# An output bias added to the residual stream beforehand by GpSimd, and a row of maxima sent ahead of a stack of parts

## The reference

```python
x = x + layernorm(attn0(layernorm(x)))            # phase one: 16 heads of 8, causal
f = layernorm(x)
for l in range(2):                                # l = 0: phase two, l = 1: phase three
    f = f + attn(ln(f, ln1[l]), wq, wk, wv, wo, bq, bk, bv, bo)   # the residual: f + y @ wo + bo
    h = ln(f, ln2[l])
    moe = token_moe if l == 0 else seq_moe        # 8 experts, the best 2 for a token / a sequence
    f = f + moe(h)
x = x + layernorm(f)
```

## Time and profile before

| | before |
|---|---|
| time, median of 3 runs | 1253.86 us (1253.05 to 1258.78) |
| the profiled execution's own time | 1253.16 us |
| its span, first to last instruction | 1251.4 us |
| TensorE's matmuls busy | 1060.6 us (85%) |
| VectorE busy | 980.6 us (78%) |
| ScalarE busy | 792.0 us (63%) |
| GpSimd busy | 685.8 us (55%) |

### The profile page before, as it was taken

One profiled execution on the slowest core, in us unless ns is written; L12 is line 12 of the kernel. 1 busy time (PEld: TensorE's weight loads), 2 busy tenths in 40 slices (PEclk: granted clock), 3 DMA queues, 4 the chain that ended last, 5 costly groups with the idle time before them and its releaser, 6 DMA issues. The chain is left out here.

```text
span 1251.4 us, 37899 instructions
## 1 busy us (share of the span) xinstructions
PE 1060.6 (85%) x10453; PEld 789.4 (63%) x10453; DVE 980.6 (78%) x2919; ACT 792.0 (63%) x1908; POOL 685.8 (55%) x1018
## 2 busy tenths in 40 slices
PE   1788999999999999999369997388889889989997
PEld 0565666666666666666269997255656556658986
DVE  3678999999998898899547765368888998876665
ACT  1566777777777767776158886256666666754554
POOL 3345555556656777776723333566676676532332
PEclk9999999999999999999679999589999899989999
DMA  5232111111111221121122222243311212100000
GB/s 144 86 110 78 50 38 42 51 52 53 53 40 45 68 66 52 55 66 43 36 72 67 69 67 74 57 116 99 85 53 53 64 39 67 53 2 10 23 18 21
DMA packets 118053, 73.07 MB, mean 58 GB/s; under 512 B 8384, under 2 KB 112960, under 8 KB 117952
## 3 DMA queue, kind: packets, MB, share of 16 engines
q1 hardware_dynamic: 99296, 53.11, 15.3%
q10 hardware_dynamic: 14560, 10.35, 3.0%
q0 software_dynamic: 4096, 8.40, 2.1%
HBM read 21.68 MB, written 11.60 MB: 27 GB/s over the span
## 5 line engine op out<-in xcount | busy, mean ns | idle before, releaser
L617 DVE TENSOR_REDUCE negm<-bank 128x2 f32<-128x512 f32 (+1 forms) x576 | 389.3, 679 | 82.0 <-PE bank L309 57.0
L505 ACT ACTIVATE prob<-bank 128x512 f32<-128x512 f32 x576 | 339.6, 595 | 127.1 <-PE bank L331 88.8
L898 POOL TENSOR_SCALAR_AFFINE_SELECT prob<-prob 128x512 f32<-128x512 f32 x384 | 248.6, 649 | 172.6 <-ACT prob L505 170.7
L350 PE MATMUL bank<-prob,vaug 128*32 128x256 f32 (+1 forms) x3072 | 168.6, 338 | 4.1 <-ACT oT L511 3.3
L1217 POOL COPY w_job<-w_s 128x512 f32 x104 | 69.1, 665 | 153.4 <-PE bank L1186 152.6
L317 PE MATMUL bank<-stack 126*128 126x256 bf16 x768 | 151.8, 279 | 0.0
L336 PE MATMUL bank<-stack 128*128 128x256 bf16 x768 | 150.8, 278 | 0.9 <-ACT prob L505 0.9
L1208 ACT ACTIVATE prob<-bank,b_job 128x128 f32<-128x128 f32 (+1 forms) x416 | 131.8, 400 | 17.2 <-PE bank L1186 9.9
L1197 PE MATMUL bank<-w_job,prob 128*128 128x128 f32 x1088 | 139.0, 276 | 2.5 <-issue 1.6
L1197 PEld LDWEIGHTS bank<-w_job,prob 128*128 128x128 f32 x1088 | 131.3, 192 | 6.4 <-issue 5.3
L350 PEld LDWEIGHTS bank<-prob,vaug 128*32 128x32 f32 x3072 | 81.5, 110 | 80.7 <-issue 48.9
(11 more groups left out here) (181 smaller groups left out, 2122.0 us busy)
## 6 DMA issues: line engine op xcount, KB each, us to landing
stack<-parts SPq DMA_DIRECT2D x288, 128.0 KB
w_s<-e_w ACTq DMA_DIRECT2D x32, 256.0 KB, 3.0
oT<-x_routed SPq DMA_DIRECT2D x72, 64.0 KB, 1.7
y_routed<-oT SPq DMA_DIRECT2D x36, 128.0 KB, 1.9
stack<-mT SPq DMA_DIRECT2D x192, 4.0 KB
out<-x_all SPq DMA_DIRECT2D x16, 128.0 KB, 1.8
b_all<-e_b ACTq DMA_DIRECT2D x2, 512.0 KB, 8.4
x_routed<-hk,x_at POOLq DMA_INDIRECT x64
```

Of the source, the lines that this page charges most:

```text
L350: m = nc.tensor.matmul(o, w, (prob0, prob1)[kb][:, g % 2, h], start=kb == 0, stop=kb == 1, skip_group_check=True)
L505: nc.scalar.activation(o, s, ACT.Exp, scale=SCALE).then_inc(exp_done, 1)
L617: nc.vector.tensor_reduce(o, s, AX.X, ALU.max, negate=True).then_inc(max_done, 1)
L898: nc.gpsimd.affine_select(out=t, in_=t, compare_op=ALU.is_ge, fill=0.0, base=0, pattern=[[0, HG], [1, P]], channel_multiplier=-1).then_inc ...
```

## The change

GpSimd gets a new instruction for each item of phases two and three, `pool_bias`, in slot 3 of the step before the item's own: it adds the output bias to the item's part of `f_all` in place. The residual of these items on VectorE becomes one instruction, PSUM plus `f_all`, in place of two. `res` is advanced by two at once, so later waits are as before. In slot 2, SP sends all six stack DMAs of an item of phases two and three after the row of maxima; for items of phase one, two still go ahead of it. The placing pieces 3, 4 and 5 move from slot 3 to the middle of slot 2, the end of slot 2 and the beginning of slot 3.

```diff
         def dve_residual(i):
 
-            base = NRES * i.v
             dve.wait_ge(o3_ps, i.v + 1)
+            if i.phase > 0:
+                dve.wait_ge(biased, i.v - B + 1)
+                nc.vector.tensor_tensor(pair(f_all, i), post_bank[:, 0:T].rearrange("p (j d) -> p j d", j=2),
+                                        pair(f_all, i), ALU.add).then_inc(res, 2)
+                return
             nc.vector.tensor_tensor(att[:, i.par], post_bank[:, 0:T].rearrange("p (j d) -> p j d", j=2),
                                     bo_s[:, i.phase:i.phase + 1].to_broadcast([P, 2, P]),
                                     ALU.add).then_inc(res, 1)
-            if i.phase > 0:
-                dve.wait_ge(res, base + 1)
-                nc.vector.tensor_tensor(pair(f_all, i), pair(f_all, i), att[:, i.par], ALU.add).then_inc(res, 1)
...
             if k == 3 and placing:
-                dve_place(first, 3)
+                dve_place(first, 5)
...
+            if k == 2 and placing:
+                dve_place(first, 3)
             if k == 2 and ranked:
                 dve_logits(oldest)
...
+            if k == 2 and placing:
+                dve_place(first, 4)
             if k == 2 and ranked:
                 dve_top(oldest, 0)
             if k == 3 and ranked:
                 dve_top(oldest, 2)
-            if k == 3 and placing:
-                dve_place(first, 4)
-            if k == 3 and placing:
-                dve_place(first, 5)
...
+        def pool_bias(i):
+
+            pool.wait_ge(xn_ok, 2 * i.v + 2)
+            alone(pool)
+            nc.gpsimd.tensor_tensor(pair(f_all, i), pair(f_all, i),
+                                    bo_s[:, i.phase:i.phase + 1].to_broadcast([P, 2, P]), ALU.add).then_inc(biased, 1)
...
             if ie:
                 pool_select(ie, ge, 1)
+            if k == 3 and nxt and nxt.phase > 0:
+                pool_bias(nxt)
...
+            ahead_of_row = 2 if nxt and nxt.phase == 0 else 0
             if k == 2 and nxt:
-                sp_stack(nxt, range(0, 2))
+                sp_stack(nxt, range(0, ahead_of_row))
             if im:
...
             if k == 2 and nxt:
-                sp_stack(nxt, range(2, 6))
-            if k == 3 and nxt:
-                sp_stack(nxt, range(6, TERMS))
+                sp_stack(nxt, range(ahead_of_row, TERMS))
```

More of the change, by code:

```diff
@@ L201, in build @@
         top, placed, rank_ps, hk_sb = sem("top"), sem("placed"), sem("rank_ps"), sem("hk_sb")
+        biased = sem("biased")
         x_sent = [sem("x_sent0"), sem("x_sent1")]
```

## The result

| | before | after |
|---|---|---|
| time, median of 4 runs each | 1255.51 us (1253.05 to 1258.78) | 1287.59 us (1285.09 to 1291.89) |
| the profiled execution's own time | 1253.16 us | 1291.89 us |
| ratio after / before, 95% interval | | 1.026 [1.022, 1.030] |

The changed kernel is slower, by 32 us in the medians and by 39 us between the two profiled executions. The sign was as forecast, the size was not: 1264 us was predicted, and the range ended at 1275.

A forecast was written before the change was run, and what follows sets the result against it. The stack was taken to bound items 15 to 20, VectorE's slot 1 items 38 to 44, both nearly items 21 to 30. Terms 7.1 + 4.9 - 4.5 + 2.2 + 2.1 - 1 = +10.8 on 1253.16 gave 1264 us, range 1250 to 1275.

The forecast's parts named there:

- SP's order decides: SP's queue, phases two and three: a step lasts the end of `mT` plus 8.05 us, unless something else is later.
- A: Items 15 to 20, six steps, bound by the stack: from 17.0 to 18.2 us each, +7.1 us.
- B: Items 21 to 30, ten steps, bound by stack and VectorE nearly at once: 18.45 us each, +4.9 us.
- D: Items 38 to 44, seven steps, bound by VectorE in slot 1: from 19.6 to 18.65 us each before a clock allowance.
- Six DMAs in 7.1 us: Step's end: from the first of six stack DMAs to TensorE's start takes 7.1 us, with bounds of 6.9 and 7.37.
- So I give 2 back: Items 38 to 44: TensorE's single stack waits of some 2 us bring half clock, cutting the gain from 6.5 to 4.5 us.
- Rival 3: Longer waits halve the clock often: from item 15 on, 0.5 us more for 20 steps, 1274 us; chance 0.13.
- Items 38 to 44, -4.5 us: VectorE's slot-1 bound goes and the stack bounds these seven steps: 4.5 us gained after 2 us given back for the clock.
- The two additions become one: VectorE's residual: one instruction of 0.41 us; VectorE gains 1.16 us in items 21 to 30, 2.18 in 38 to 44.
- GpSimd's bias costed at nothing: End of GpSimd's slot 3: the new addition takes 0.58 us, none on the path; uncovered, 19 us over 32 items.
- Placing at nothing: Small instructions moved about one slot forward from the end of slot 3 cost nothing, in time VectorE has freed.
- C, +2.2 us: Items 32 to 37, six steps while second-layer expert weights load: 19.9 us a step, 119.4 in all, 2.2 us slower.

The follow-up runs named there:

- e1: The kernel before with SP's new order alone, all six stack DMAs after the row in phases two and three: 1310.09 us, ratio 1.043.
- e2: The changed kernel with SP's old order, two stack DMAs ahead of the row for every item: 1257.82 us, ratio 1.002.
- e3: The changed kernel with seven filler matmuls before TensorE's wait for the stack in phases two and three: 1270.76 us, ratio 1.012.
- e5: e2 with six filler matmuls before TensorE's wait for the row of group 1 in phases two and three: 1259.35 us, ratio 1.005.
- e11: The changed kernel without GpSimd's bias, which is left out of the output for phases two and three: 1288.92 us, ratio 1.026.
- e8: e5 without GpSimd's bias, which is left out of the output for phases two and three: 1252.11 us, ratio 0.999.
- e4: The kernel before with GpSimd's bias and the joined residual alone, SP's order and placing pieces as before: 1259.63 us, ratio 1.004.
- e6: The changed kernel with one stack DMA ahead of the row in phases two and three, in place of none: 1255.20 us, ratio 1.000.
- e12: The changed kernel with the bias behind GpSimd's fetches, SP's old order, and six filler matmuls before the row wait, items 22 to 44: 1247.17 us, ratio 0.992.

## Why the prediction was right in its sign and wrong in its size

**SP's order decides: right.** e1 and e2 show it from both sides. With the old order the change makes no difference, with the new order alone it loses 54 us. The form of the step, `mT` plus row plus six DMAs, held in every step of A, B and D.

**Six DMAs in 7.1 us: mis-sized.** They took 7.58 on average, near the 7.37 of the earlier trace rows, which I had as the upper bound. I had taken the value from four DMAs plus two issues. With the clock kept (e3) they took 7.36 over the same steps, so the half clock explains about half of the excess and no more. With a row to first DMA that took 0.92 to 1.3 us in most steps of B and D instead of 0.75, set against an earlier `mT` (9.97 for 10.4, 10.49 for 10.6), this makes e3's span, at full clock, 5.8 us longer than my forecast's, and 7.8 without the 2 us that I had given for the clock. The Trainium skill's figure ("DMA: Bandwidth & Descriptors", Anatomy of one DMA), by which I had estimated about 6.2 us for six, was further off than the rows. It stands there for DMAs that GpSimd issues, which my prediction did not say, and these are SP's.

**"So I give 2 back": this is the step that failed.** I priced the half clock in D alone and at 2 us, where e3's filler alone takes back 16.8 us, most of it in B and C. The row to look at was my own: I wrote that TensorE would wait for the stack about 2 us in one piece and that waits of this size had come with the half clock, and then let that count in one stretch, although the same wait stood at the end of every step from A on. Rival 3 had the mechanism, at 0.5 us for 20 steps; it was 1.6 us for some ten, and with the DMAs' longer time it carries the result past the range. Its "against", that item 17 waited and ran at 1.00, rested on a wait of 0.61 us, which says nothing of waits of 2. None of my signs of being wrong watched the clock.

**Items 38 to 44, -4.5 us: +3 off, and for another reason than I gave.** They gained 1.4. The seven steps were to lose a bound by VectorE. Item 42 in the kernel before shows that there was none: 18.78 us with the blocked L675 in it, at full clock. What D had to gain was the half clock of five of its steps, and the changed kernel won most of that back (0.94 to 0.99), while the stack cost it 0.3 us a step.

**The two additions become one: right** as a duration, 0.415 us in all 32 cases, never blocked. The rule that the Trainium skill gives ("SBUF — State Buffer", Who interferes with whom) agrees with this, and again with the combine in e5, which has two inputs in SBUF and stretched from 0.62 to 1.89 us for two beside GpSimd's L920.

**GpSimd's bias costed at nothing: right in the changed kernel, wrong beyond it.** e11 measures nothing there, e8 measures 7 us with the old order. It was 0.72 us rather than 0.58, and what the waits for `y_got` in e5 and e8 point to is the fetch behind it in its queue, not the next step's parts. I had named sends and fetches as queued behind it and not followed who waits for them.

**Placing at nothing: right**, as far as e4 against e2 can tell.

**C, +2.2 us: mis-sized** for the same two reasons, 11.4 in the event, of which 8.1 went away with e3's filler. **The drain, -1:** the rest of the span is 0.4 longer and not shorter.

Left open: why in B the first stack DMA leaves 1.29 us after the row in some steps, where nothing in the queue stands between; why waits of 1.96 us and more went with half clock at ten steps of the five stretches and not at two others, while in e2 shorter ones, from 1.62 us, were enough; and what in the six DMAs takes the time that four did not show.

## What to carry to other kernels

Before you put a small transfer ahead of a large one in a queue, look at what the small one is waiting for, because the large one will wait for it too: here two of six DMAs could leave 1.2 us earlier than the row, and holding them back cost 54 us over 31 steps (e1). With one of them left ahead (e6) the changed kernel's loss was gone. When a forecast says that TensorE will wait in one piece, multiply by the steps and price the slower clock behind each of those waits, from the longest waits of the trace and not from its average ones. And when an instruction that was blocked is made fast, compare steps that ran with and without the slower clock before booking its time as a gain.

## What the runs showed of the hardware

- The granted clock fell to 1.2 GHz with ten waits of 1.96 to 5.83 us for the stack in the changed kernel, and in e2 also behind waits from 1.62 us for the row. One such stretch made a slot of 4.65 us into one of 6.23. Six or seven matmuls whose result nobody reads, placed before the wait, kept the clock at 1.00 in B and D (e3, e12; in C it was 0.94 and 0.95) and were worth 16.8 us in e3.
- Splitting a wait in two did the same as filling it: with one DMA moved (e6), no wait of D for row or stack was over 1.3 us, and D ran at a clock of 1.00 and 18.8 us a step without any filler.
- GpSimd's addition of 128x256 with a broadcast input took 0.72 us, the one of 128x512 1.16: half the elements, 62% of the time.
- With the old order and VectorE's stall gone the times spread more: 1252 to 1268 us in e2 and 1254 to 1272 in e4, where the kernel before spread over 1251 to 1260 on the same chip, one execution of 2761 us aside. With one DMA ahead (e6) they spread over 1253 to 1260. What differs from one execution to the next is not shown, as each kernel has one trace.
